# Graph attention on one core: the nodes of the last four tiles added by VectorE and stored with plain transfers from SyncE's queue

## The chip, the core and the metric

The kernel is one program on one NeuronCore of a Trainium2 chip. The metric is device time in microseconds (us), the median of several executions. Four engines compute (TensorE, VectorE = DVE, ScalarE = ACT, GpSimd = POOL); SyncE (SP) only waits and issues transfers. Transfers are issued by SP, ACT and POOL and are carried by the core's 16 DMA engines.

## The reference

One graph attention layer over N = 6144 nodes with 512 features and 8 heads of 64:

```
h    = relu(layernorm(x))
hW   = h @ W                              # per head
s1, s2 = hW . a1, hW . a2                 # per node and head
att  = softmax over neighbours m (adj[n, m] > 0) of leaky_relu(s1[n] + s2[m], 0.2)
out  = x + elu(att @ hW)                  # x: the nodes as they came in
```

The adjacency is a 6144 x 6144 int32 matrix (151 MB). Few edges are set, most of them in the first rows and columns. The last line matters here: each row of the result is elu(...) plus the node row x that came in.

## The kernel before, in words

The 6144 nodes are 48 tiles of 128 rows. A first block (`project_and_scan`) normalises and projects all tiles, writes the table of projected rows to DRAM, and scans the adjacency of tiles 0 to 29 for the edges of each row. ACT packs each half tile of the adjacency to bytes (`pack`, L243), DVE searches the bytes. Half tiles lie in six buffers of 1.5 MB, `adj_rows0` to `adj_rows5`; SP loads the next one when ACT has packed the one before (`load_adj`, semaphore `checked`). A short block (`plan`) follows, then `attend_edges`, in which the last three buffers are given up: buffers 0 to 2 serve the rest of the scan (tiles 30 to 47), the last half tiles being packed by ACT around 590 to 610 us. `flag` and a conditional end the program.

`attend_edges` works in units of one or two tiles (`UNITS`; `GROUPED` are those that finish a tile, numbered g). For each unit POOL gathers node rows from the table by indirect DMA (L975, L980), DVE scores and weighs them (L1126 to L1141), PE sums them (L1279 to L1287), and then the group is finished in this order: `normalise` on DVE (L1148, L1153), `grow` on ACT (L1031, L1033), `finish` on DVE (L1161), which signals `bent`. `finish` of one unit stands on DVE ahead of `normalise` of the next. `result` has four slots, taken in turn.

How x gets into the result depends on the tile (`add_x` on POOL, `store` on ACT):

- For tiles in `COPIED` (0 to 21, and the pair 46, 47) the node rows were copied from x to the output in DRAM during the scan, by SP (`copy_nodes`, L215, one copy every second round, the twelfth being that of 46 and 47). After `bent`, POOL issues one accumulating transfer of `result` onto the output (L962).
- For the tiles 22 to 45, POOL issues after `bent` an accumulating transfer of x onto `result` (L964), and when it has landed ACT stores `result` with a plain transfer (L1040).

At the end SP waits until all the results have landed (L995, L996); each engine then drains, they meet, and the flag is read (L1557). The marks L879, L731, L484 and L368 are those of the ends of the four blocks, where all engines meet.

Of the kernel before, what the change touches and what calls it, by code (L numbers as in the profile page):

```python
# [18 lines left out]
F32 = mybir.dt.float32  # L19
BF16 = mybir.dt.bfloat16  # L20
I32 = mybir.dt.int32
ALU = mybir.AluOpType
# [8 lines left out]
HF = H * F  # L31
TILES = N // P
# [13 lines left out]
EARLY = 30  # L46
HALF = N // 2
COPY_TILES, COPY_ROWS = 2, 8
COPIED = tuple(range(0, 22, COPY_TILES)) + (46,)
PACK = 4  # L50


# [81 lines left out]
def make_units():  # L134
    units, v, group = [], 0, 0
    while v < len(VISITS):
        a = VISITS[v]
        b = VISITS[v + 1] if v + 1 < len(VISITS) else a
        alike = (a.direct, a.rest, a.kind) == (b.direct, b.rest, b.kind) and 2 * (a.direct + a.rest) <= WIDEST
        whole = a.first and a.last and b.first and b.last  # L140
        n = 2 if alike and b is not a and (whole or a.tile == b.tile) else 1
        units.append(Unit(list(range(v, v + n)), group))
        group += units[-1].last
        v += n
    return units


UNITS = make_units()
U = len(UNITS)
GROUPED = [u for u in UNITS if u.last]  # L150
# [37 lines left out]
def buffer_of(i):  # L188

    return i % 6 if i < 2 * EARLY else (i - 2 * EARLY) % 3  # L190


def occupant(i):

    return max((k for k in range(i) if buffer_of(k) == buffer_of(i)), default=None)
# [16 lines left out]
def copy_nodes(queue, sb, x, out, t):  # L212

    rows = slice(t * P, (t + COPY_TILES) * P)
    queue.dma_start(out[rows].rearrange("(p r) d -> p (r d)", r=COPY_ROWS),  # L215
                    x[rows].rearrange("(p r) d -> p (r d)", r=COPY_ROWS)).then_inc(sb["copied"], 16)


def lies_in_output(unit):

    return all(t - t % COPY_TILES in COPIED for t in range(unit.tile, unit.tile + unit.tiles))


def load_adj(sp, sb, adj, i):

    u, t = buffer_of(i), i // 2
    if occupant(i) is not None:
        sp.wait_ge(sb["checked"], occupant(i) + 1)
        if occupant(i) < 2:
            sp.wait_ge(sb["keyed"], 1)  # L230
    sp.dma_start(sb["adj_rows"][u][:], adj[t * P:(t + 1) * P, i % 2 * HALF:(i % 2 + 1) * HALF]).then_inc(sb["adj_loaded"][u], 16)
# [234 lines left out]
def project_and_scan(nc, sb, x, adj, table, out):  # L466
# [17 lines left out]
    with ExitStack() as ctx:  # L484
# [27 lines left out]
        def _(sp):  # L512
            for t in range(TILES):
# [6 lines left out]
                for i in range(6, 2 * EARLY + 3):  # L520
                    if act_round[occupant(i)] == t:
                        load_adj(sp, sb, adj, i)
                if t % 2 == 0 and 1 <= t // 2 <= len(COPIED):
                    copy_nodes(sp, sb, x, out, COPIED[t // 2 - 1])
            sp.wait_ge(h_copied, TILES)
# [327 lines left out]
def attend_edges(nc, sb, x, adj, table, out):  # L853
# [25 lines left out]
    with ExitStack() as ctx:  # L879
        def buf(name, shape, dtype=F32):  # L880
            return ctx.enter_context(nc.sbuf_tensor(name, shape, dtype))
# [4 lines left out]
        def sem(name):  # L886
            return ctx.enter_context(nc.semaphore(name))
# [10 lines left out]
        score = buf("score", [P, 3, BLOCKS, H])  # L898
        recip, agg = buf("recip", [P, 2, H]), buf("agg", [P, 2, 2, HF])
        result = buf("result", [P, 4, 2, HF])  # L900
        used, degree, half, listed, empty = (buf(n, [P, LV] + more) for n, more in (
            ("late_used", [SLOTS["C"]]), ("late_degree", []), ("late_half", []), ("late_listed", []), ("late_empty", [])))
        rising, late_sums, worst, flag_f = buf("late_rising", [P, LV, DIRECT]), buf("late_sums", [P, LV]), buf("worst", [P, 1]), buf("flag_f", [1, 1])
# [3 lines left out]
        x_added, stored, laid = ([sem(f"{n}{u}") for u in range(4)] for n in ("x_added", "out_stored", "out_added"))  # L907
# [7 lines left out]
        recips, bent = sem("recips"), sem("bent")  # L915
        late_step, late_counted, late_placed, late_planned = sem("late_step"), sem("late_counted"), sem("late_placed"), sem("late_planned")
        worst_ready, worst_summed, late_cleared = sem("worst_ready"), sem("worst_summed"), sem("late_cleared")
        block = ctx.enter_context(nc.Block())
        xt = x.rearrange("(t p) d -> p t d", p=P)
        ot = out.rearrange("(t p) d -> p t d", p=P)  # L920
        def out_written(g):

            return 16 * sum(lies_in_output(v) == lies_in_output(GROUPED[g]) for v in GROUPED[g % 4:g + 1:4])
# [25 lines left out]
        @block.gpsimd  # L949
        def _(pool):  # L950
            nc.gpsimd.iota(edge_no[:], [[1, longest * P]], base=0, channel_multiplier=0, allow_small_or_imprecise_dtypes=True).then_inc(made, 1)
            nc.gpsimd.iota(list_no[:], [[P, longest]], base=0, channel_multiplier=1, allow_small_or_imprecise_dtypes=True).then_inc(made, 1)
            nc.gpsimd.memset(rising[:], 0.0).then_inc(late_cleared, 1)

            def add_x(g):

                w, o = GROUPED[g], g % 4
                pool.wait_ge(bent, g + 1)
                if lies_in_output(w):
                    if g == 0:  # L960
                        pool.wait_ge(sb["copied"], 16 * len(COPIED))
                    nc.gpsimd.dma_start(ot[:, w.tile:w.tile + w.tiles], result[:, o, 0:w.tiles], accum_op=ALU.add).then_inc(laid[o], 16)  # L962
                else:
                    nc.gpsimd.dma_start(result[:, o, 0:w.tiles], xt[:, w.tile:w.tile + w.tiles], accum_op=ALU.add).then_inc(x_added[o], 16)  # L964
            for u, w in enumerate(UNITS):
                k = u % AHEAD
                if u >= AHEAD:
                    pool.wait_ge(shifted, u - AHEAD + 1)
                if node_old[u] >= 0:
                    pool.wait_ge(summed, node_old[u] + 1)  # L970
                if u == late:
                    pool.wait_ge(late_planned, 1)
                for i, v in enumerate(w.parts):
                    for j in range(w.direct):
                        nc.gpsimd.indirect_dma_start(out=nodes[:, node_at[u] + i * w.direct + j], out_offset=None, in_=table,  # L975
                                                     in_offset=bass.IndirectOffsetOnAxis(ap=sb["column"][:, v, j:j + 1], axis=0)
                                                     ).then_inc(gathered[k], 16)
                pool.wait_ge(columns, u + 1)
                for q in range(w.rests):
                    nc.gpsimd.indirect_dma_start(out=nodes[:, node_at[u] + w.directs + q], out_offset=None, in_=table,  # L980
                                                 in_offset=bass.IndirectOffsetOnAxis(ap=column[:, k, q:q + 1], axis=0)
                                                 ).then_inc(gathered[k], 16)
                if u >= 4 and UNITS[u - 4].last:
                    add_x(UNITS[u - 4].group)
            for u in range(U - 4, U):
                add_x(UNITS[u].group)

        @block.sync
        def _(sp):
            for u in range(U):  # L990
                for i in range(2 * EARLY + 3, 2 * TILES):
                    if max(0, act_round[i - 3 - 2 * EARLY]) == u:
                        load_adj(sp, sb, adj, i)
            for k in range(4):
                sp.wait_ge(stored[k], 16 * sum(not lies_in_output(w) for w in GROUPED[k::4]))  # L995
                sp.wait_ge(laid[k], 16 * sum(lies_in_output(w) for w in GROUPED[k::4]))  # L996

        @block.scalar
        def _(act):
# [33 lines left out]
                nc.scalar.activation(result[:, o, 0:w.tiles], result[:, o, 0:w.tiles], ACT.Exp, scale=-1.0).then_inc(grown_done, 1)  # L1033
            def store(u):

                if u < 0 or not UNITS[u].last or lies_in_output(UNITS[u]):
                    return
                g, w = UNITS[u].group, UNITS[u]
                act.wait_ge(x_added[g % 4], out_written(g))
                act.dma_start(ot[:, w.tile:w.tile + w.tiles], result[:, g % 4, 0:w.tiles]).then_inc(stored[g % 4], 16)  # L1040
# [26 lines left out]
            for u in range(U - 4, U):  # L1067
                store(u)

        @block.vector  # L1070
        def _(dve):
# [86 lines left out]
            def finish(g):  # L1158
                w, o = GROUPED[g], g % 4
                dve.wait_ge(grown_done, g + 1)  # L1160
                nc.vector.scalar_tensor_tensor(result[:, o, 0:w.tiles], result[:, o, 0:w.tiles], -1.0, agg[:, g % 2, 0:w.tiles],  # L1161
                                               ALU.add, ALU.max).then_inc(bent, 1)
            steps = [0]

            def did(ins):
# [336 lines left out]
def build(nc, x, adj, W, a1, a2, out):  # L1502
    table = nc.dram_tensor("table", (N + 2, TABLE), F32).ap()
    s2_rows = nc.dram_tensor("s2_rows", (H, N), F32).ap()
    with ExitStack() as ctx:
# [5 lines left out]
        with ExitStack() as edges:  # L1511
# [29 lines left out]
            with ExitStack() as scan:  # L1541
# [12 lines left out]
                project_and_scan(nc, sb, x, adj, table, out)  # L1554
                plan(nc, sb, table)
            attend_edges(nc, sb, x, adj, table, out)
        flag = nc.values_load(sb["flag"][0:1, 0:1], min_val=0, max_val=1, skip_runtime_bounds_check_because="a comparison wrote it")  # L1557
        with nc.If(flag > 0):
# [28 lines left out]
```

## Time and profile before

| what | us |
|---|---|
| median of 3 runs | 791.15 (789.62 to 793.73) |
| span of the profiled execution, the one time shown of it | 794.7 |
| DVE busy | 650.7 (82%) |
| PE busy | 571.2 (72%) |
| ACT busy | 477.0 (60%) |
| POOL busy | 422.1 (53%) |

The span runs from the first to the last instruction of the profiled execution. It lies 3.6 us above the median of the runs and 1.0 us above the slowest of them. Mean granted clock of TensorE 0.845. Read the busy shares with care: they are means over blocks with different limits, and what this change touches lies in a few places: one transfer in the first block, one load near 594 us, and the last 25 us.

### The profile page before, as it was taken

The page shows a single profiled execution, that of the slowest core. Times are in us where ns is not written, and L with a number is a line of the kernel's source. Part 1 is how long each engine was busy: PE and PEld are TensorE (multiplying, and loading weights), DVE is VectorE, ACT ScalarE, POOL GpSimd, SP SyncE. Part 2 cuts the span into 40 slices and gives each one's busy share as a digit, 9 for nine tenths or more (in the row PEclk, how much of TensorE's full clock was granted, in tenths as well). Part 3 has the DMA queues.
Part 4 walks back from the last instruction along what each step waited for, and adds up shares of the span by engine and source line. Part 5 has one row for each costly group of instructions (what it writes and reads, how often), then busy time and mean ns, then how long its engine had stood idle before and what let it go on. Part 6 is the DMA issues. An engine that isn't in the chain of part 4 may idle for free.

```text
span 794.7 us, 9122 instructions
## 1 busy us (share of the span) xinstructions
PE 571.2 (72%) x2182; PEld 405.8 (51%) x2182; DVE 650.7 (82%) x1967; ACT 477.0 (60%) x761; POOL 422.1 (53%) x804
## 2 busy tenths in 40 slices
PE   0389789898888688833868768687766759877860
PEld 0245455454445344423646557565655548766650
DVE  4659988999866776944959999999979988999771
ACT  0678797799889989515735566666545223333321
POOL 4634444453333333126756457647666776888720
PEclk9989999999888887955769889777878779999895
DMA  9999999999999999716999999999997877899985
GB/s 289 415 383 416 376 373 392 392 401 419 416 419 422 420 421 419 288 32 217 404 404 401 409 401 400 394 396 402 397 398 236 219 208 172 225 259 281 302 210 133
DMA packets 62171, 269.50 MB, mean 339 GB/s; under 512 B 12066, under 2 KB 12066, under 8 KB 49636
## 3 DMA queue, kind: packets, MB, share of 16 engines
q1 hardware_dynamic: 32484, 184.24, 57.5%
q0 software_dynamic: 26368, 78.36, 32.9%
q10 hardware_dynamic: 3264, 6.29, 2.1%
q8 instruction: 19, 0.31, 0.2%
q14 instruction: 36, 0.29, 0.1%
HBM read 243.49 MB, written 31.66 MB: 346 GB/s over the span
## 4 chain that ended last, share of the span: by engine, by line
DVE 28%; issue 8%; DMA 7%; POOL 6%; ACT 3%; PE 2%; POOLq 0%; DVEq 0%; ACTq 0%
DVE nodes L1141 11%; DMA nodes<-table,list_column 6%; DVE places L264 4%; POOL nodes L980 4%; DVE best L253 3%; DVE agg L1153 3%; POOL nodes L975 2%; ACT result L1031 1%; ACT result L1033 1%; DVE to_row L1117 1%; DMA out_dram<-result 1%; DVE result L1161 1%; DVE owner L1082 1%; DVE infoC L285 1%; DVE chosen L1098 1%
## 5 line engine op out<-in xcount | busy, mean ns | idle before, releaser
L666 PE MATMUL psH<-sb_W,normedT 128*128 128x512 f32 x384 | 229.6, 689 | 0.0
L243 ACT ACTIVATE packed<-adj_rows,eight 128x3072 uint8<-128x3072 int32 x66 | 188.8, 2860 | 0.8
L975 POOL DMA_INDIRECT nodes<-table,column x138 | 137.1, 993 | 64.3 <-issue 39.7
L713 POOL TENSOR_TENSOR sb_node_sum<-sb_node_sum,h_rows 128x512 f32<-128x512 f32 x48 | 61.2, 1276 | 153.4 <-ACT h_rows L631 153.3
L980 POOL DMA_INDIRECT nodes<-table,list_column x109 | 108.7, 998 | 63.0 <-DVE list_column L1106 33.4
L1279 PE MATMUL psP<-nodes,ident 128*128 128x256 f32 x276 | 104.0, 464 | 53.1 <-issue 42.8
L1141 DVE TENSOR_TENSOR nodes<-nodes,psW 128x2048 f32<-128x2048 f32 (+4 forms) x66 | 138.6, 2141 | 0.0
L667 PEld LDWEIGHTS psS<-sb_Wa,normedT 128*128 128x128 f32 x384 | 79.9, 208 | 106.0 <-issue 106.0
L264 DVE FIND_INDEX8 places<-best,packed 128x8 uint32<-128x96 f32 (+6 forms) x240 | 109.8, 465 | 0.0
L253 DVE MAX8 best<-packed 128x8 f32<-128x96 f32 (+6 forms) x240 | 102.6, 458 | 6.4 <-ACT packed L243 6.4
L1280 PE MATMUL psP<-nodes,ident 128*128 128x264 f32 x276 | 101.0, 453 | 0.0
L1279 PEld LDWEIGHTS psP<-nodes,ident 128*128 128x128 f32 x276 | 61.1, 233 | 67.5 <-issue 52.7
L658 PE MATMUL psT<-ident,normed 128*128 128x128 f32 x192 | 35.2, 312 | 76.6 <-ACT normed L615 76.6
L243 ACT ACTIVATE packed<-sb_adj_rows,eight 128x3072 uint8<-128x3072 int32 x30 | 86.7, 2889 | 0.1
L1031 ACT ACTIVATE result<-agg 128x1024 f32<-128x1024 f32 (+1 forms) x29 | 26.4, 909 | 89.0 <-DVE agg L1153 83.6
L1286 PE MATMUL psP<-nodes,to_row 128*128 128x256 f32 x218 | 72.7, 418 | 7.1 <-DVE nodes L1141 7.1
L1287 PE MATMUL psP<-nodes,to_row 128*128 128x264 f32 x218 | 71.2, 411 | 0.0
L1280 PEld LDWEIGHTS psP<-nodes,ident 128*128 128x128 f32 x276 | 63.5, 230 | 12.1
L666 PEld LDWEIGHTS psH<-sb_W,normedT 128*128 128x128 f32 x384 | 65.2, 213 | 0.0
L658 PEld LDWEIGHTS psT<-ident,normed 128*128 128x128 f32 x192 | 24.2, 162 | 79.6 <-ACT normed L615 79.6
L667 PE MATMUL psS<-sb_Wa,normedT 128*128 128x16 f32 x384 | 59.5, 231 | 0.0
L1286 PEld LDWEIGHTS psP<-nodes,to_row 128*128 128x128 f32 x218 | 45.4, 212 | 19.4 <-DVE nodes L1141 11.0
(179 smaller groups left out, 885.3 us busy)
## 6 DMA issues: line engine op xcount, KB each, us to landing
adj_rows<-in_adj_dram SPq DMA_DIRECT2D x66, 1536.0 KB, 10.2
sb_adj_rows<-in_adj_dram SPq DMA_DIRECT2D x30, 1536.0 KB, 12.5
table<-h_rows SPq DMA_DIRECT2D x48, 260.0 KB, 8.8
sb_x_rows<-in_x_dram SPq DMA_DIRECT2D x48, 256.0 KB, 9.0
out_dram<-in_x_dram SPq DMA_DIRECT2D x12, 512.0 KB, 11.1
result<-in_x_dram POOLq DMA_DIRECT2D x12, 512.0 KB, 7.9
out_dram<-result ACTq DMA_DIRECT2D x12, 512.0 KB, 4.9
out_dram<-result POOLq DMA_DIRECT2D x7, 512.0 KB, 6.7
```

The costliest lines, as they stand in the source:

```text
L243: nc.scalar.activation(words.bitcast(mybir.dt.uint8), sb["adj_rows"][buffer_of(i)][:], ACT.Square, bias=sb["eight"][:], scale=-17.0, accum ...
L253: ins = nc.vector.max(sb["best"][:, t % 2, 8 * n:8 * n + 8], sb["packed"][:, t % 2, lo:hi])
L264: ins = nc.vector.max_index(sb["places"][:, t % 2, 8 * n:8 * n + 8], sb["best"][:, t % 2, 8 * n:8 * n + 8], sb["packed"][:, t % 2, lo:hi])
L666: nc.tensor.matmul(psH[:, t % 2], normedT[:, t % 2, kc], sb["W"][:, kc], start=(kc == 0), stop=(kc == KC - 1))
L667: mm = nc.tensor.matmul(psS[:, t % 2, 0:2 * H], normedT[:, t % 2, kc], sb["Wa"][:, kc], start=(kc == 0), stop=(kc == KC - 1))
L975: nc.gpsimd.indirect_dma_start(out=nodes[:, node_at[u] + i * w.direct + j], out_offset=None, in_=table, in_offset=bass.IndirectOffsetOnAxi ...
L980: nc.gpsimd.indirect_dma_start(out=nodes[:, node_at[u] + w.directs + q], out_offset=None, in_=table, in_offset=bass.IndirectOffsetOnAxis(a ...
L1141: nc.vector.tensor_tensor(rows, rows, psW[:, lo:hi].unsqueeze(3).to_broadcast([P, hi - lo, H, F]), ALU.mult).then_inc(weighted, 1)
L1279: nc.tensor.matmul(low, sb["ident"][:], nodes[:, n, 0:LOW], start=a, stop=False)
L1280: nc.tensor.matmul(high, sb["ident"][:], nodes[:, n, LOW:TABLE], start=a, stop=False)
L1286: nc.tensor.matmul(low, to_row[:, u % TURNS, r], nodes[:, n, 0:LOW], start=False, stop=z)
L1287: mm = nc.tensor.matmul(high, to_row[:, u % TURNS, r], nodes[:, n, LOW:TABLE], start=False, stop=z)
```

## The change

The pair 46, 47 is taken out of `COPIED`; SP makes one copy fewer in the first block. The last four tiles (44 to 47, two groups) are `kept`. SP waits until buffer 0 of the adjacency has been packed for the last time and loads x of these four tiles into it (`x_kept`, 1 MB). In `finish`, DVE does the old instruction and then, after waits on that load and on the old instruction, adds `x_kept` to `result`; only then does it signal `bent`. For these two groups POOL's `add_x` and ACT's `store` do nothing; SP waits for `bent` and stores `result` with a plain transfer.

```
-COPIED = tuple(range(0, 22, COPY_TILES)) + (46,)
+COPIED = tuple(range(0, 22, COPY_TILES))
+KEPT = 4
+def kept(unit):
+    return unit.tile >= TILES - KEPT
...
+        x_kept = sb["adj_rows"][0][:, 0:KEPT * HF].bitcast(F32).rearrange("p (t d) -> p t d", t=KEPT)
...
             def add_x(g):
                 w, o = GROUPED[g], g % 4
+                if kept(w):
+                    return
...
+            sp.wait_ge(sb["checked"], 1 + max(i for i in range(2 * TILES) if buffer_of(i) == 0))
+            sp.dma_start(x_kept, xt[:, TILES - KEPT:TILES]).then_inc(x_here, 16)
+            for g, w in enumerate(GROUPED):
+                if kept(w):
+                    sp.wait_ge(bent, g + 1)
+                    sp.dma_start(ot[:, w.tile:w.tile + w.tiles], result[:, g % 4, 0:w.tiles]).then_inc(stored[g % 4], 16)
...
-                if u < 0 or not UNITS[u].last or lies_in_output(UNITS[u]):
+                if u < 0 or not UNITS[u].last or lies_in_output(UNITS[u]) or kept(UNITS[u]):
...
-                nc.vector.scalar_tensor_tensor(result[:, o, 0:w.tiles], result[:, o, 0:w.tiles], -1.0, agg[:, g % 2, 0:w.tiles],
-                                               ALU.add, ALU.max).then_inc(bent, 1)
+                ins = nc.vector.scalar_tensor_tensor(result[:, o, 0:w.tiles], result[:, o, 0:w.tiles], -1.0, agg[:, g % 2, 0:w.tiles],
+                                                     ALU.add, ALU.max)
+                if not kept(w):
+                    ins.then_inc(bent, 1)
+                    return
+                ins.then_inc(bare, 1)
+                first = w.tile - (TILES - KEPT)
+                dve.wait_ge(x_here, 16)
+                dve.wait_ge(bare, 1 + sum(kept(v) for v in GROUPED[:g]))
+                nc.vector.tensor_tensor(result[:, o, 0:w.tiles], result[:, o, 0:w.tiles], x_kept[:, first:first + w.tiles],
+                                        ALU.add).then_inc(bent, 1)
```

## Rows read from the trace of the kernel before

**Rows 1.** Timeline of DVE, last 25 us (start us, us, engine, line, operation)

```profile
771.44 1.22 DVE L1161 SCALAR_TENSOR_TENSOR result<-result,agg 128x1024 f32<-128x1024 f32 x1 [2.21 <-ACT result L1033]
773.94 0.26 DVE L1148 RECIPROCAL recip<-psP 128x16 f32<-128x16 f32 x1 [1.28 <-PE psP L1287]
774.24 1.29 DVE L1153 TENSOR_TENSOR agg<-psP,recip 128x512 f32<-128x512 f32 x2
...
777.73 1.23 DVE L1161 SCALAR_TENSOR_TENSOR result<-result,agg 128x1024 f32<-128x1024 f32 x1 [2.21 <-ACT result L1033]
```

**Rows 2.** Timeline of POOL, last 25 us

```profile
764.73 1.19 POOL L964 DMA_DIRECT2D result<-in_x_dram  x1 [6.30 <-DVE result L1161]
772.96 1.19 POOL L964 DMA_DIRECT2D result<-in_x_dram  x1 [7.04 <-DVE result L1161]
779.42 1.22 POOL L962 DMA_DIRECT2D out_dram<-result  x1 [5.26 <-DVE result L1161]
```

**Rows 3.** DMA issues, 779 to 781 us (KB each, us from issue to landing)

```profile
out_dram<-result POOLq DMA_DIRECT2D x1, 512.0 KB, 6.7
```

**Rows 4.** Line L879, end of the block, by engine (ns min/median/max, first and last start us)

```profile
L879 POOLq EVENT_SEMAPHORE  x2: 17/17/17, 790.2 to 790.2; - x2
...
L879 POOLq DRAIN  x1: 10722/10722/10722, 779.4 to 779.4; - x1
...
L879 SPq DRAIN  x1: 7/7/7, 786.4 to 786.4; - x1
```

**Rows 5.** Line L731, end of the block of `plan`, where POOL drained early

```profile
L731 POOLq EVENT_SEMAPHORE  x2: 17/17/17, 352.5 to 352.6; - x2
...
L731 POOLq DRAIN  x1: 872/872/872, 341.8 to 341.8; - x1
...
L731 SPq COMPARE_BRANCH  x1: 33/33/33, 352.3 to 352.3; - x1
```

**Rows 6.** Stretches: length, busy us by engine, clock, DMA share, GB/s

```profile
776.50:777.00 0.50, 0.00 (x0) 0.00 (x0) 0.00 (x0) 0.47 (x2) 0.00 (x0) 1.00 1.17 213
...
780.00:780.50 0.50, 0.00 (x0) 0.00 (x0) 0.00 (x0) 0.00 (x0) 0.50 (x1) 0.50 1.03 385
...
786.20:794.70 8.50, 0.00 (x0) 0.00 (x0) 0.00 (x0) 0.00 (x0) 0.00 (x0) 0.50 0.01 3
```

**Rows 7.** ACT's stores L1040, all twelve: us from issue to landing

```profile
DMA to landing us min/median/max: 2.8/4.9/8.3
```

**Rows 8.** Timeline of ACT, last 25 us

```profile
776.65 1.98 ACTq L1040 DMA_DIRECT2D out_dram<-result  x3
```

**Rows 9.** DMA issues, 776 to 777 us

```profile
out_dram<-result ACTq DMA_DIRECT2D x1, 512.0 KB, 2.9
```

**Rows 10.** Timeline of ACT, the packing of the last half tile in buffer 0

```profile
594.26 0.18 ACT L243 ACTIVATION_READ_ACCUMULATOR packed<-adj_rows,eight 128x1 f32 x1
```

**Rows 11.** The stretch behind it

```profile
595.00:600.00 5.00, 2.68 (x16) 2.01 (x14) 4.90 (x9) 2.64 (x8) 3.68 (x3) 1.00 1.03 353
```

**Rows 12.** DMA issues, 585 to 590 us

```profile
nodes<-table,list_column POOLq DMA_INDIRECT x2, 13.6
```

**Rows 13.** Timelines of POOL and DVE: gathers issued, and the scores

```profile
585.69 0.95 POOL L980 DMA_INDIRECT nodes<-table,list_column  x1 [0.31 <-issue]
...
579.95 0.24 DVE L1126 TENSOR_TENSOR score<-nodes,sides 128x80 f32<-128x80 f32 x1 [4.76 <-DMA nodes<-table,list_column]
...
611.39 0.21 DVE L1126 TENSOR_TENSOR score<-nodes,sides 128x64 f32<-128x64 f32 x1
```

**Rows 14.** Waits, 170 to 340 us (engine, line, releaser: total us, times, longest)

```profile
ACT h_rows L629 <- PE psS L667: 17.4, 6, 4.5
DVE stats L535 <- DMA sb_x_rows<-in_x_dram: 9.0, 5, 2.5
```

**Rows 15.** The copies L215, and a stretch of the first block behind the twelfth

```profile
L215 SPq DMA_DIRECT2D out_dram<-in_x_dram x12: 522/527/788, 51.7 to 177.6; - x12
...
200.00:210.00 10.00, 7.22 (x21) 4.08 (x20) 8.64 (x28) 9.61 (x17) 5.10 (x16) 0.72 1.03 424
```

More of the change, by code:

```diff
@@ L917, in attend_edges @@
         worst_ready, worst_summed, late_cleared = sem("worst_ready"), sem("worst_summed"), sem("late_cleared")
+        x_here, bare = sem("x_here"), sem("bare")
         block = ctx.enter_context(nc.Block())
```

## The prediction

> **What bounds the kernel now.** The page comes first: DVE is the busiest engine, but with 82% of the span it isn't the bound everywhere, so I look at each place that the change touches by itself. The last 25 us come next, read from the timelines of DVE and POOL. The last `finish` starts on DVE at 777.73 and takes 1.23 us, so it ends at 778.96 [rows 1]. POOL issues the accumulating store at 779.42, which is 0.46 us later [rows 2], and it lands 6.7 us after that [rows 3], at 786.1. SP, which waited for it, is at its drain at 786.4 [rows 4].
>
> What the reader should see now is in the end of the block. SP is done at 786.4, yet the block is left only at 790.2: POOL posts its two meeting events there, right where its drain ends, since 779.4 + 10.7 = 790.1 [rows 4]. In between no engine computes and the DMA engines move 3 GB/s [rows 6]. Nobody but POOL is late. At the end of `plan`, where POOL had drained ten microseconds early (341.8 + 0.9), POOL posts at 352.5, that is 0.2 us behind SP's last branch at 352.3 [rows 5]. So POOL's drain behind its last transfer costs 790.2 - 786.5 = 3.7 us here, on top of the transfer. That the drain is long because a transfer of POOL's own queue is still out is a reading of one case: it starts with the last accumulating transfer, and the other drain was short with none out.
>
> **The end of the program, step by step.** (1) *Added:* DVE's addition of 128x1024 f32 in the last `finish`. The trace has no addition of that shape; the nearest row is the instruction before it, same shape, two inputs, 1.23 us [rows 1]. Between dependent instructions DVE leaves 0.04 us (773.94 + 0.26 to 774.24) [rows 1], so the result is ready at 778.96 + 0.04 + 1.23 = 780.23 instead of 778.96. Cost 1.27 us, all of it on the path. Nothing is taken off this bound from below; from above it is one more reaction between engines, 0.4 us.
>
> (2) *Replaced:* POOL's 0.46 us of reaction and the 6.7 us of its transfer, by a plain store that SP issues. SP stands in the wait for `bent` with nothing else queued ahead; I give it 0.1 us, so issue at 780.33. ACT's twelve stores of the same size took 2.8 to 8.3 us to land, median 4.9 [rows 7]; the one at 776.65 took 2.9 [rows 8, 9]. What separates them is how busy the DMA engines are. ACT's last three stores go out between 776.65 and 778.63 [rows 8]; in the new kernel they are two, 1 MB, at about 385 GB/s [rows 6] some 2.7 us, so they are through at about 780.5, when SP's data has not begun. I take 2.85 us: landing at 783.18. Bounds 2.8 and 8.3.
>
> (3) *Landing to release:* SP's own steps were 786.1 to 786.4, and POOL's post lay 0.2 us behind SP's last branch in the other block [rows 5]; 0.4 us in all. Release at 783.6, if POOL is not late.
>
> (4) *Gone:* POOL's last transfer is now the one at 764.73 [rows 2]. If its drain again lasts 10.7 us, it ends at 764.7 + 10.7 = 775.4, some 8 us ahead of SP. So the 3.7 us of [rows 4] go too. Bounds of this term: 0 (something else holds POOL to a few us behind the last landing) and 3.7; I take 3.7, because nothing of POOL is left to wait for.
>
> Release at 783.6 against 790.2: **-6.6 us**. Of this the transfer gives 786.1 - 783.2 = 2.9 and the drain 3.7. What follows the release (794.7 - 790.2 = 4.5 us, flag and branch) is the same.
>
> Why 2.85 and not 6.7 again: at a full DMA share the engines move 213 GB/s at 776.5, when the accumulating load issued at 772.96 is all that is out, and 385 at 780.0, when ACT's plain stores are [rows 2, 6, 8]. The kind of transfer counts, then, and so does that it stands behind nothing; the queue by itself isn't the reason. The Trainium skill, page "DMA: Bandwidth & Descriptors", section "Issuing engines are not separate DMA queues", says that DMAs from SP, ACT and POOL run on the same 16 engines and that issuing them from several engines saves only sequencer time. By that rule, taken alone, the store would land 6.7 us after its issue here too, and the transfer's gain of 2.9 would turn into a loss of about 0.9.
>
> **The other edits.** *Addition of the group before* (tiles 44, 45). It stands on DVE ahead of the last `normalise`. The old instruction ends at 772.66, the reciprocal starts at 773.94, released by PE [rows 1]. The hole is 1.28 us, the addition with its gap 1.27. Cost 0; if PE came earlier, up to 1.27. Of the same group, POOL's transfer of x at 772.96 [rows 2] and ACT's third store go; SP stores at about 774, long before the end.
>
> *The load of x_kept.* Buffer 0 is packed for the last time and its sum read by 594.26 + 0.18 = 594.44 [rows 10]; SP, which has no adjacency left to load, then asks for 1 MB. The DMA engines are full there, 353 GB/s at a share of 1.03 [rows 11], so 1 MB at 400 GB/s pushes other transfers by up to 2.6 us. Who needs them? The gathers issued before 594 are the ones next in use: that of 585.69 landed within about 13.6 us, at 599.3, and its unit is scored at 611.39 [rows 12, 13]. Twelve us of slack cover 2.6. Taken 0, bound +2.6. The data itself is needed only at 772.7.
>
> *The copy that is dropped.* 0.5 MB less to carry at about 178 us, 0.53 us of SP's issue [rows 15]. At 424 GB/s that is 1.2 us of a full DMA system. But DMA isn't what the scan waits for: ACT is busy 9.61 of 10 us there, its waits between 170 and 340 us are for PE (17.4 us), and only DVE's statistics wait for a load of x, 9.0 us in five pieces [rows 14, 15], with DVE not full (8.64 of 10). Taken 0, bound -1.2.
>
> Sum: -6.6 us on the span of 794.7, that is 788.1. The profiled execution lies 3.6 us above the median of the runs; I take the difference over to the median: 791.15 - 6.6 = 784.5 (0.83% faster).
>
> **The rivals.** About 0.5%, 4.0 us here, is what a measurement of this kernel can tell from no change; the three runs shown spread by 4.1.
>
> A. *POOL stays last.* What keeps POOL until 790.2 isn't its own transfer but whatever lands last, so it still posts 790.2 - 786.1 = 4.1 us behind it. Then the release is at 783.2 + 4.1 = 787.3, gain 2.9, median 788.2: no change to be told. For it: the drain has one example. Against it: SP's drain at that place takes 7 ns [rows 4], and POOL's in `plan` had ended long before SP did [rows 5]. Chance 0.13.
>
> B. *The store lands no faster.* Price 6.7 us instead of 2.85: release 780.33 + 6.7 + 0.4 = 787.4, gain 2.8, median 788.3. The Trainium skill's section on issuing engines, named above, speaks for it. So does that ACT's stores did take up to 8.3 us (release at 789.0, gain 1.2) [rows 7]. Against it: that one met other traffic, and ACT's two stores are through by 780.5. Chance 0.10.
>
> C. *The load of x_kept delays the gathers* (the other side). The row at 579.95 shows DVE 4.76 us idle for a gather under full DMA [rows 13], so late gathers do reach the path. To cancel 6.6 us the load must push the gather by its slack and that, 12 + 6.6 = 18.7 us, and by 22.7 to be slower by over 0.5%; its fair price is 2.6. Should it happen, some 796. Chance 0.05.
>
> D. *The dropped copy is worth its 1.2 us as well:* 783.3. Chance 0.15.
>
> The forecast itself, 784.5 with a us or so either way, 0.57. Faster by over 0.5%: forecast and D, 0.72, plus a little of A and B with a quick store, 0.73. Within 0.5%: A, B and those rounding towards it, 0.21. Slower: C and what I don't see, 0.06. The range reaches down to D with a us of the runs' own scatter, 782.0, and up through A and B with some, 789.0.
>
> **What the profile would show.** POOL's drain of line L879 starts near 766 and ends before 777, and POOL posts within 0.3 us of SP. SP issues two stores of `result`, near 774 and 780.3, landing in about 2.9 us. DVE has a second instruction of about 1.23 us in the last two `finish`, and the last reciprocal still starts when PE releases it. No new wait on gathers after 594 us. Wrong would be: POOL's post 4 us behind SP's drain (A), a landing of 5 us or more (B), DVE idle for gathers between 600 and 640 us (C), or a span that differs from 794.7 already ahead of 760 us.

## The result, and the profile after

The changed kernel takes 785.4 us (median of 20 runs, 779.76 to 790.09) against 793.07 us before (20 runs, 788.75 to 801.01): ratio 0.9899, 95% interval 0.988 to 0.9919, so 1.0% faster, 6.4 to 9.5 us. The forecast was 784.5 us from a median of 791.15, a gain of 6.6.

The profiled execution has a span of 783.6 us against 794.7. That is 11.1 us less, more than the 7.7 by which the medians differ, so the stretches have to be read one by one. Part of it is the execution that was profiled: in all the runs of which both are known the device time lies 1.5 to 2.0 us above the span, so the profile of before stands for an execution of some 796.5 us (an estimate), 3.4 above its median, while that of the changed kernel took 785.17 us, close to its median. DVE's timeline over the last group (start us, us):

```profile
767.47 1.23 DVE L1177 SCALAR_TENSOR_TENSOR result<-result,agg 128x1024 f32<-128x1024 f32 x1 [2.21 <-ACT result L1049]
768.80 1.23 DVE L1186 TENSOR_TENSOR result<-result,adj_rows 128x1024 f32<-128x1024 f32 x1
769.94 0.25 DVE L1164 RECIPROCAL recip<-psP 128x16 f32<-128x16 f32 x1
...
773.73 1.23 DVE L1177 SCALAR_TENSOR_TENSOR result<-result,agg 128x1024 f32<-128x1024 f32 x1 [2.21 <-ACT result L1049]
775.06 1.23 DVE L1186 TENSOR_TENSOR result<-result,adj_rows 128x1024 f32<-128x1024 f32 x1
```

These answer to [rows 1]. The addition takes 1.23 us as estimated, and starts 0.10 us behind the instruction before it (773.73 + 1.23 to 775.06), where the forecast had 0.04. The last reciprocal stands right behind the addition of the group before: no wait for PE is noted at it any more. SP's timeline, and its last issue in the view of DMA issues from 776 to 777 us:

```profile
591.47 0.38 SPq L1005 DMA_DIRECT2D adj_rows<-in_x_dram  x1
770.05 6.64 SPq L1009 DMA_DIRECT2D out_dram<-result  x2
```

```profile
out_dram<-result SPq DMA_DIRECT2D x1, 512.0 KB, 2.8
```

The merged row of the two stores ends at 776.69, and an issue takes 0.38 us, so the last one starts at 776.31, within 0.1 us of the end of the addition. It lands 2.8 us later, at 779.1; [rows 3] showed 6.7. Now the end of the block, the answer to [rows 4]:

```profile
L885 POOLq EVENT_SEMAPHORE  x2: 17/17/17, 779.3 to 779.4; - x2
L885 POOLq DRAIN  x1: 11147/11147/11147, 760.7 to 760.7; - x1
...
L885 SPq COMPARE_BRANCH  x1: 33/33/33, 779.1 to 779.1; - x1
L885 SPq DRAIN  x1: 7/7/7, 779.3 to 779.3; - x1
```

POOL's drain is as long as before, 11.1 us, but it begins at 760.7 and is over at 771.9. POOL posts at 779.3 to 779.4, right behind SP. From the start of the last reciprocal to POOL's last post it is 779.4 - 769.94 = 9.5 us; before it was 790.2 - 773.94 = 16.3. So 6.8 of the 11.1 us lie there. Another 0.3 lie behind the post (4.2 us in place of 4.5), and 4.0 ahead of the last reciprocal. Whether these 4.0 belong to the change was open, and the experiments had to settle it.

### The profile page after: what moved, and what is told of

It reads as the page before. It is cut to its first block, busy times and chain, and to the rows that moved or that the text cites. A ratio compares the mean times of both kernels' runs of the same rounds, so it can differ in the third digit from the quotient of the medians.

```text
span 783.6 us, 9125 instructions
## 1 busy us (share of the span) xinstructions
PE 568.1 (73%) x2182; PEld 405.0 (52%) x2182; DVE 650.9 (83%) x1969; ACT 477.8 (61%) x761; POOL 421.9 (54%) x802
## 4 chain that ended last, share of the span: by engine, by line
DVE 23%; DMA 10%; POOL 9%; issue 9%; ACT 4%; PE 0%; DVEq 0%; POOLq 0%
DVE nodes L1157 9%; DMA nodes<-table,list_column 9%; POOL nodes L990 5%; POOL nodes L985 3%; DVE agg L1169 3%; DVE places L270 2%; ACT result L1049 2%; ACT result L1047 2%; DVE best L259 2%; DVE to_row L1133 1%; DVE result L1177 1%; DMA nodes<-table,column 1%; DVE owner L1098 1%; POOL out_dram L972 1%; PE psC L1288 0%
## 5 line engine op out<-in xcount | busy, mean ns | idle before, releaser
L672 PE MATMUL psH<-sb_W,normedT 128*128 128x512 f32 x384 | 223.0, 672 | 0.0
L1304 PE MATMUL psP<-nodes,ident 128*128 128x256 f32 x276 | 108.1, 481 | 49.5 <-issue 43.2
L673 PEld LDWEIGHTS psS<-sb_Wa,normedT 128*128 128x128 f32 x384 | 78.1, 203 | 102.1 <-issue 102.1
L1305 PE MATMUL psP<-nodes,ident 128*128 128x264 f32 x276 | 104.0, 465 | 0.0
L1304 PEld LDWEIGHTS psP<-nodes,ident 128*128 128x128 f32 x276 | 62.9, 240 | 64.5 <-issue 49.3
L1311 PE MATMUL psP<-nodes,to_row 128*128 128x256 f32 x218 | 71.5, 412 | 6.6 <-DVE nodes L1157 6.6
L1305 PEld LDWEIGHTS psP<-nodes,ident 128*128 128x128 f32 x276 | 65.8, 238 | 13.4
## 6 DMA issues: line engine op xcount, KB each, us to landing
adj_rows<-in_adj_dram SPq DMA_DIRECT2D x66, 1536.0 KB, 10.9
```

Source lines behind the costliest of these rows:

```text
L672: nc.tensor.matmul(psH[:, t % 2], normedT[:, t % 2, kc], sb["W"][:, kc], start=(kc == 0), stop=(kc == KC - 1))
L673: mm = nc.tensor.matmul(psS[:, t % 2, 0:2 * H], normedT[:, t % 2, kc], sb["Wa"][:, kc], start=(kc == 0), stop=(kc == KC - 1))
L1304: nc.tensor.matmul(low, sb["ident"][:], nodes[:, n, 0:LOW], start=a, stop=False)
L1305: nc.tensor.matmul(high, sb["ident"][:], nodes[:, n, LOW:TABLE], start=a, stop=False)
L1311: nc.tensor.matmul(low, to_row[:, u % TURNS, r], nodes[:, n, 0:LOW], start=False, stop=z)
```

## The experiments

All ratios are against the kernel before, measured beside each run. "Tail" is the time from the start of the last reciprocal on DVE to POOL's last post, both read from the run's profile. What follows the post takes 4.1 to 5.4 us in these profiles, 4.5 and 5.2 in the two of before; the expectations that count from the last `finish` to the end of the program carry this scatter.

| run | ratio (95%) | tail, us |
|---|---|---|
| before | 1 | 16.3 |
| before again | one execution | 785.6 - 768.56 = 17.0 |
| changed | 0.9899 (0.988 to 0.9919) | 9.5 |
| e1 copy back | 0.9915 (0.9883 to 0.9946) | 780.9 - 771.40 = 9.5 |
| e2 last pair only | 0.9922 (0.9894 to 0.995) | 776.1 - 765.88 = 10.2 |
| e3 POOL plain store | 0.9969 (0.9948 to 0.9991) | 786.2 - 771.51 = 14.7 |
| e4 small late POOL transfer | 0.9982 (0.9954 to 1.0009) | 788.0 - 773.53 = 14.5 |
| e5 ACT store | 0.9897 (0.9862 to 0.9933) | 780.7 - 770.75 = 10.0 |
| e6 add ahead | 0.9895 (0.9849 to 0.9942) | 773.7 - 765.02 = 8.7 |
| e7 add ahead, halves | 0.9897 (0.9868 to 0.9925) | 781.6 - 772.44 = 9.2 |
| e8 no node load | 0.9869 (0.9838 to 0.9899) | 776.3 - 766.91 = 9.4 |
| e10 last pair by load | 0.9994 (0.9964 to 1.0024) | 786.8 - 770.20 = 16.6 |
| e11 add ahead, SP stores | 0.987 (0.9824 to 0.9916) | 777.8 - 769.64 = 8.2 |
| e12 halves, SP stores | 0.9852 (0.9811 to 0.9894) | 771.7 - 764.47 = 7.2 |

The theory: the gain comes from the tail alone, and there from two things, a plain transfer in place of an accumulating one, and a POOL whose last transfer is long over. Rivals: the queue, not the kind of transfer; the dropped copy; the node load as a cost.

**e3, the plain stores issued by POOL**

```
-                    sp.wait_ge(bent, g + 1)
-                    sp.dma_start(ot[...], result[...]).then_inc(stored[g % 4], 16)
...
+                pool.wait_ge(bent, g + 1)
+                if kept(w):
+                    nc.gpsimd.dma_start(ot[...], result[...]).then_inc(pool_stored, 16)
```

> The changed kernel with the two plain stores issued by POOL in place of SP. Theory: the kind of transfer sets the landing, so it lands in 2.8 to 4 us from its issue, but POOL's drain is back behind it, 10.7 us from the start of that transfer; tail from the last finish about 0.45 + 2.5 + 10.7 + 4.3 = 18 us, against 17.0 before and 9.9 after; ratio 1.000 to 1.002. Rival, that the queue sets the landing: 6.7 us from the issue. Rival, that the drain comes with accumulating transfers alone: tail 11 to 12 us, ratio 0.992.

POOL's timeline, its DMA issue and the end of the block in this run:

```profile
778.16 0.73 POOL L968 DMA_DIRECT2D out_dram<-result  x1 [5.51 <-DVE result L1184]
```

```profile
out_dram<-result POOLq DMA_DIRECT2D x1, 512.0 KB, 3.2
```

```profile
L885 POOLq EVENT_SEMAPHORE  x2: 17/17/17, 786.1 to 786.2; - x2
L885 POOLq DRAIN  x1: 7945/7945/7945, 778.1 to 778.1; - x1
...
L885 SPq DRAIN  x1: 7/7/7, 781.6 to 781.6; - x1
```

Both of POOL's plain stores land in 3.2 us, where SP's took 2.8 in the changed kernel: the kind of transfer sets the landing, the queue adds 0.4. SP is through at 781.6, but POOL's drain ends at 778.1 + 7.9 = 786.1 and holds everybody 4.5 us. So the drain comes with a plain transfer as well. It lasted 7.9 us though, not 10.7: the drain does not have a fixed length. The expected 18 us from the last `finish` were 15.1, and the ratio is 0.9969 where 1.000 to 1.002 was expected. The run also splits the gain. Of the 6.8 us by which the tail shrank, 1.6 came with the plain transfer from POOL (issued 0.1 us sooner behind the last instruction and landing in 3.5 us less, against 1.3 for the addition and 0.7 for a longer drain); the other 5.2 came only when the last transfer was no longer POOL's.

**e4, one small late transfer of POOL**

```
+            pool.wait_ge(bent, len(GROUPED))
+            nc.gpsimd.dma_start(scrap, result[:, 0, 0, 0:16]).then_inc(scrapped, 16)
```

> The changed kernel, and behind the last addition POOL issues one transfer of 8 KB to a scrap tensor; everything else as in the changed kernel. Theory, drain counted from the issue: it ends 10.7 us after the start of this transfer, tail from the last finish about 18 us, ratio 1.000. Rival, drain counted from the landing (before: 790.1 against 786.1, 4.0 us): the small transfer lands in 2 us, tail 0.45 + 2.5 + 2 + 4 + 4.3 = 13.3 us, ratio 0.994. If a transfer so small leaves no drain: tail 10 us, ratio 0.990.

```profile
out_dram<-result SPq DMA_DIRECT2D x1, 512.0 KB, 2.9
scrap<-result POOLq DMA_DIRECT2D x1, 8.0 KB, 2.8
```

```profile
L885 POOLq EVENT_SEMAPHORE  x2: 17/17/17, 787.9 to 788.0; - x2
L885 POOLq DRAIN  x1: 7728/7728/7728, 780.1 to 780.1; - x1
...
L885 SPq DRAIN  x1: 7/7/7, 783.2 to 783.2; - x1
```

8 KB land in 2.8 us (first fence, DMA issues), nearly with SP's 512 KB, and cost the program 787.9 - 783.2 = 4.7 us (second fence, end of the block). The ratio goes from 0.990 back to 0.998. Neither theory had the number: from the last `finish` to the end of the program it takes 793.4 - 777.3 = 16.1 us, between the 18 and the 13.3 of the two. A drain of 10.7 us from the issue is out, since this one lasts 7.7. Counted from the landing, 780.17 + 2.8 = 783.0, it ends 4.9 us behind: the rival has the form right, and each of its terms too small (landing 2, drain 4, and 4.3 behind the post, where 5.4 were measured).

**e2, only tiles 46 and 47 kept**

```
-KEPT = 4
+KEPT = 2
```

> The changed kernel with only tiles 46 and 47 kept; 44 and 45 get x by POOL's accumulating load and are stored by ACT as before. POOL's last transfer is then issued when the finish of 44 and 45 ends, some 0.4 us after it, about 7.1 us ahead of the end of the last addition. Theory that POOL's drain takes 10.7 to 11.1 us from the start of its last transfer, whatever that carries: POOL posts about 0.6 us later than SP alone would let it, tail from the last finish 10.3 to 10.6 us, ratio 0.990 to 0.991. Rival, that the drain ends 4 us behind the landing: POOL is done before SP, tail 9.9 us or up to 0.5 longer for the late store of ACT, ratio 0.990.

The end of the block:

```profile
L885 POOLq DRAIN  x1: 9425/9425/9425, 765.1 to 765.1; - x1
...
L885 SPq DRAIN  x1: 7/7/7, 776.0 to 776.0; - x1
```

POOL's last accumulating load starts at 765.1 and lands 5.5 us later; its drain lasts 9.4 us and is over at 774.5, SP is at its drain at 776.0. The rival held: the drain follows the landing, by 3.9 us here, and POOL was not late. What the tail gained in length, 10.2 against 9.5, is SP's store landing in 3.5 us; ACT's third store, issued 1.7 us ahead of it, is still out. So traffic of that kind costs a plain store 0.7 us, and does not explain 6.7. The ratio, 0.9922, cannot tell the run from the changed kernel.

**e5, the stores issued by ACT**

```
+                if kept(w):
+                    act.wait_ge(bent, g + 1)
+                else:
                     act.wait_ge(x_added[g % 4], out_written(g))
```

> The changed kernel with the two plain stores issued by ACT, behind its other stores, in place of SP. Theory: the kind of transfer counts and POOL's freedom, not that it is SP; the last store lands in 2.8 to 3.5 us, tail from the last finish 9.9 to 10.6 us, ratio to before 0.990 to 0.991. Rival, that SP's queue by itself is what is quicker: landing 4 to 5 us (the median of ACT's stores was 4.9), ratio 0.992 to 0.993.

Landing 3.3 us, tail 10.0, ratio 0.9897. SP's queue is nothing special. ACT's drain starts at 777.5, right behind the issue of its last store, and takes 0.15 us, although that store lands only at 780.4: a long drain behind a transfer of its own is seen at POOL, not at ACT. The Trainium skill, page "DMA: Bandwidth & Descriptors", section "Issuing engines are not separate DMA queues", says that the same 16 engines carry what any engine issues; on the landing the runs agree with it (2.8, 3.2 and 3.3 us from SP, POOL and ACT).

**e10, the kernel before without the twelfth copy**

```
-COPIED = tuple(range(0, 22, COPY_TILES)) + (46,)
+COPIED = tuple(range(0, 22, COPY_TILES))
```

> The kernel before with the last pair taken out of the copied tiles and nothing else: POOL adds x onto the result by an accumulating load and ACT stores it, as for tiles 22 to 45. Theory, drain behind POOL's last transfer: POOL's last transfer starts at the same place as before, lands in 5.4 us, its drain ends 4 to 5 us behind that; ACT's store lands 2.9 us behind the load and isn't last; from the last reciprocal to POOL's post 15 to 16.3 us, ratio 0.998 to 1.000. Rival: the end is what lands last plus a fixed time; then the chain of two transfers makes it 17 to 18 us, ratio 1.001 to 1.003.

```profile
L879 POOLq DRAIN  x1: 11036/11036/11036, 775.6 to 775.6; - x1
...
L879 SPq DRAIN  x1: 7/7/7, 785.7 to 785.7; - x1
```

Its tail is 16.6 us, a little over what was expected, because POOL's load, which starts at 775.67, lands 7.0 us later and not 5.4. The drain ends at 775.6 + 11.0 = 786.7 (end of the block), again 4.0 behind that landing. ACT's store lands after POOL's load, at 785.5, so the drain follows POOL's own last transfer and not what lands last; it holds the program for 1.0 us behind SP. Ratio 0.9994: a load and a plain store one after the other take as long as the accumulating store with its drain, and gain nothing. The run also lacks the twelfth copy, and no gain of that is seen; but it changes two things at once, and the copy by itself is the subject of e1.

**e1, the copy put back into the changed kernel**

```
-                if t % 2 == 0 and 1 <= t // 2 <= len(COPIED):
+                if t % 2 == 0 and 1 <= t // 2 <= len(COPIED) + 1:
...
```

> The changed kernel with the twelfth copy (x of tiles 46 and 47 to the output, in DRAM, during the scan) put back; its data are overwritten at the end. Theory: the copy is hidden in the scan, the time stays that of the changed kernel, ratio to before 0.990, and the tail from the last finish on takes 9.9 us as in the changed kernel. Rival: the 3.6 us by which the first block ended earlier in the profile of the changed kernel are the copy's; then this kernel is 1.2 to 3.6 us slower than the changed one, ratio 0.992 to 0.995.

Tail 9.5, ratio 0.9915: 0.0016 above the changed kernel, well inside both intervals. From the last `finish` to the end of the program it takes 10.9 us, not 9.9; the difference lies behind the post. The first score, at 373.25 us, comes 3.8 us later than in the changed kernel, as the rival would have it, but kernels without the copy have it as late (e9, below). A cost of the copy of up to 1.2 us, the forecast's bound, is not excluded.

**e9, the kernel before once more**

> The kernel before, once more, for the scatter of a profile. Theory: what stands between the last reciprocal and POOL's post is set by fixed steps, so it comes out at 16.3 us again to within half a us, with a drain of POOL of some 10.7 us; the start of the attention block and the stretch from 650 to 745 us, in which the first profile of before lies up to 5 and 2 us behind the other kernels, scatter by as much. Rival: these differences belong to the kernel before and come again (first score at 374.8 us, 94.5 us from the score at 650.3 to that at 744.8).

```profile
L879 POOLq EVENT_SEMAPHORE  x2: 17/17/17, 785.5 to 785.6; - x2
L879 POOLq DRAIN  x1: 11473/11473/11473, 774.0 to 774.0; - x1
...
L879 SPq DRAIN  x1: 7/7/7, 781.7 to 781.7; - x1
```

SP is at its drain at 781.7 and POOL posts 3.8 us later, as in the first profile (the end of the block). The last reciprocal starts at 768.56, where it was 773.94: 5.4 us of scatter between two executions of one kernel, ahead of the tail. The tail itself is 17.0, 0.7 more, a little outside what was expected, because POOL's store landed in 7.5 us. So the 4.0 us by which the changed kernel was ahead at its last reciprocal are no effect that needs a cause: 769.94 lies between the two. Against this second profile the span of the changed kernel is 7.2 us shorter, which is the tail's 7.5 and what scatters around it. The first score tells the same: it starts at 374.80 us in the first profile of before, at 372.18 in this one, at 369.44 in the changed kernel, and at 373.92 in e10, which has the same scan as the changed kernel. Over the eleven profiles without the twelfth copy it lies between 366.6 and 374.6, over the three with it between 372.2 and 374.8.

**e8, without the load of x_kept**

```
-            sp.dma_start(x_kept, xt[:, TILES - KEPT:TILES]).then_inc(x_here, 16)
...
-                dve.wait_ge(x_here, 16)
```

> The changed kernel without the load of x into the adjacency buffer: DVE adds what the buffer holds, so the last four tiles of the output lack their nodes. Theory: the load is hidden behind gathers with some 12 us of slack; ratio 0.990 as in the changed kernel, and no stretch between 590 and 640 us gets shorter. Rival: 1 MB at a full DMA share pushes gathers by up to 2.6 us and they reach the path; then this kernel is up to 2.6 us faster than the changed one, ratio 0.987.

Ratio 0.9869, 0.003 below the changed kernel, with intervals that overlap. That is the rival's number, so the times alone lean to a load that costs some 2 us. The profiles don't: the stretch in which the load is under way is no shorter without it. From the score at 576.96 to that at 648.24 it takes 71.3 us in the changed kernel; the same stretch takes 71.5 in e8 (572.21 to 643.67), 70.4 in before (579.95 to 650.32) and 70.4 in e10, all three without the load, and 70.1 to 71.5 in the nine other kernels that have it. DVE waits once for a gather there, 0.9 us with the load (at 593.27) and 1.0 without (at 588.64). The load itself took 11.3 us to land. So the gain of e8's times has no place in its trace, and the load is hidden as far as the traces go.

**e6, e7, e11, e12: the rest of the tail.** The changed kernel suggested a better one. With elu(a) = max(a, 0) + (exp(min(a, 0)) - 1), x can be added to max(a, 0) while ACT computes the exponential:

```
+    nc.vector.scalar_tensor_tensor(x_kept[...], agg[...], 0.0, x_kept[...], ALU.max, ALU.add).then_inc(bare, 1)      # in normalise
-    ins = nc.vector.scalar_tensor_tensor(result, result, -1.0, agg, ALU.add, ALU.max)                               # in finish
-    nc.vector.tensor_tensor(result, result, x_kept, ALU.add).then_inc(bent, 1)
+    nc.vector.scalar_tensor_tensor(result, result, -1.0, x_kept[...], ALU.add, ALU.add).then_inc(bent, 1)
```

> The changed kernel with x added ahead: while ACT computes the exponential, DVE makes max(agg, 0) + x, and the last instruction is (exp - 1) plus that; as many DVE instructions as in the changed kernel, one of them off the path. Theory: the second addition lies whole on the path that sets the end, 1.3 us; the last instruction's end to the end of the program stays, tail from the last finish 8.5 us, ratio 0.988 to 0.989. Rival, that the store is held by something else (ACT's two stores ahead of it in the DMA engines): it lands later from its issue by as much as it is issued earlier, tail 9.9, ratio 0.990.

The tail fell by 0.8 us, not 1.3: the store landed in 3.2 us. The rival has its share, then. The ratio, 0.9895, shows nothing of it. e7 also takes the last group in two halves of the features:

```
+            for k in range(2):
+                part = slice(k * LOW, (k + 1) * LOW)
...
+                    sp.wait_ge(half_bent, k + 1)
+                    sp.dma_start(ot[..., part], result[..., part]).then_inc(half_stored, 16)
```

> As the run with x added ahead, and the last group is normalised, grown, finished and stored in two halves of the features, so that DVE, ACT and the DMA engines overlap. Estimate from the rows: the chain from the last reciprocal to the last landing is 1.3 + 2.2 + 1.2 + 2.8 = 7.5 us in one piece and about 0.7 + 2.6 + 0.7 + 2.3 = 6.3 us in halves; ratio 0.987. Rival: each half pays the fixed part of its instructions and its transfer (rows of 1 KB in place of 2 KB), and nothing is left of it, ratio 0.988 to 0.989.

Tail 9.2 and ratio 0.9897, where 0.987 was expected: the halves won nothing over e6. Their stores landed in 3.4 and 4.3 us beside ACT's stores of tiles 40 to 43 (the 3.9 in the expectation of e12 is the mean of the two). So ACT's stores were moved to SP, which issues them as soon as their x is in:

```
+            for u in (U - 4, U - 3):
+                sp.wait_ge(x_added[g % 4], out_written(g))
+                sp.dma_start(ot[:, w.tile:w.tile + w.tiles], result[:, g % 4, 0:w.tiles]).then_inc(stored[g % 4], 16)
```

> As the run with x added ahead, in one piece, and SP also stores tiles 40 to 43, as soon as their x has landed, in place of ACT behind its last exponential. Theory: the last store of the run with x added ahead landed in 3.2 us because ACT's two stores were still in the DMA engines; here it finds them empty and lands in 2.8 us; from the last reciprocal to POOL's post 8.3 us against 9.5 in the changed kernel, ratio 0.988 to 0.989. Rival: 3.2 us again, 8.7.

> As the run with x added ahead and the last group in halves, and SP also stores tiles 40 to 43 as soon as their x has landed. Theory: in the run in halves the two stores of 256 KB landed in 3.4 and 3.9 us behind ACT's two, which cost what the halves won; with empty DMA engines they land in 2.0 to 2.4 us, and from the last reciprocal to POOL's post it is 7.3 to 7.8 us, ratio 0.987 to 0.988. Rival: a store of 256 KB takes no less than one of 512 KB, 2.8 us; then 8.2.

The last store of e11 landed in 2.8 us, each of the two halves of e12 in 2.2 (DMA issues of e12, around 769 us):

```profile
out_dram<-result SPq DMA_DIRECT2D x1, 256.0 KB, 2.2
```

Tails 8.2 and 7.2, about as expected. e12 has the lowest time of all, 780.87 us, ratio 0.9852; that it beats the changed kernel is plain in the tail (2.3 us), while the intervals of the two ratios still overlap.

## Why the prediction was right

- *The addition, 1.27 us on the path.* Measured 775.06 + 1.23 - (773.73 + 1.23) = 1.33. Right. The gap of 0.10 us in place of 0.04 goes with the wait for the load: e8, which lacks that wait, has 0.03.
- *Store in 2.85 us behind 0.1 us of reaction.* 2.8 and less than 0.1. Right, and for the reason given: e3 and e5 show that a plain store lands in 3.2 to 3.3 us whoever issues it. Rival B is out. That the new store stands behind little is the smaller part: loads that accumulate onto `result` landed in 5.3 to 5.7 us with nearly nothing else out (before at 772.96, e2, e9) and in 7.0 behind ACT's stores (e10), a plain store in 2.8 and 3.5 (e2).
- *Release 0.4 us behind the landing, 3.7 us of drain gone.* 779.1 to 779.4, and no drain in between. Rival A is out: POOL does not wait for what lands last. e3 and e4 put the drain back, by 4.5 and 4.7 us, and in e10 it follows POOL's own last transfer although ACT's store lands later.
- The reading of the drain behind that step was too simple. "If its drain again lasts 10.7 us" gave nearly the right place by luck, since the two transfers happen to land in about the same time (6.7 and 7.2 us): the drain lasts as long as POOL's last transfer is out, and 3.9 to 4.9 us more. In the changed kernel that is 760.75 + 7.2 + 3.9 = 771.9, 7.4 us ahead of SP, a margin that would have covered the error.
- *Addition of the group before, cost 0.* It ends at 768.80 + 1.23 = 770.03 and the reciprocal starts at 769.94 with no idle time noted, where the forecast had it released by PE still. PE's last sums end at 769.14 + 0.61 = 769.75, so the addition overran the hole by up to 0.2 us; that lies ahead of the tail. Right to within this.
- *Node load and dropped copy, 0 each.* Not contradicted: the traces show no cost of the load, and e10 and e1 no effect of the copy, of which up to 1.2 us stays open in the times. The slack of twelve us was that of the gather behind, though: in the changed kernel the load went out at 591.47, while the gather for the score at 593.27 was still out, and that one had no slack (DVE waited 0.9 us for it). Only the like wait of e8 shows that this was not the load's doing. Rival C did not happen, D is not shown.
- *The sum.* Forecast 6.6 us, the tails say 6.8 (7.5 against the second profile of before), the medians 7.7, the ratio 6.4 to 9.5. Counted from the last reciprocal, the landing comes 3.0 us sooner (forecast 2.9), and the post follows it 3.8 us more closely (forecast 3.7). What the profile's span lost beyond that, 4.0 us ahead of the last reciprocal, lies inside the 5.4 us between two profiles of the kernel before. The prediction had named a difference ahead of 760 us as a sign of being wrong; one profile of each kernel cannot carry that sign. That the time itself, 785.4 against 784.5, came so close has a share of luck: the median of three runs from which it was counted lay 1.9 us below that of twenty, and the gain was 1.1 us larger than forecast.

## What to carry to other kernels

The end of a block is set by the engine that drains last, which need not be the one whose data land last: compare the time at which each engine starts and ends its drain with the time of the common post. Give the last transfer of a block to an engine whose drain was short in the profile (here SP and ACT), and let the engine with the long one finish its transfers early. When the spans of two profiles differ by more than the medians, measure from a common event near the change before looking for a cause upstream.

## What the runs showed of the hardware

- POOL's drain ended 3.9 to 4.0 us behind the landing of its last transfer in all twelve profiles in which that transfer accumulates, among them before (786.1 to 790.1), e2 (770.6 to 774.5) and e10 (782.7 to 786.7), and 4.7 to 4.9 us behind that of a plain one in e3 (781.4 to 786.1) and e4 (783.0 to 787.9). SP's, which starts when all has landed, took 7 ns in all of them, ACT's 0.15 us in e5 with its own store still out. What POOL does in that time no row shows.
- A transfer of 8 KB from POOL took as long to land as one of 512 KB from SP that was out at the same moment, 2.8 and 2.9 us. What it takes alone no run shows.
- A store of 512 KB that accumulates onto DRAM landed in 6.7 and 7.5 us at the end of the program, with ACT's plain stores still out; a plain one of 512 KB that was issued last landed in 2.8 to 3.5.
